# New places for all stages in the engines' orders of a two-layer kernel

## The reference, cut to what matters

```python
xn = layernorm(x)
x = x + cosformer(xn) + ffn0(xn)    # 16 heads of 8; linear attention
                                    # ffn0: 2 shared experts of width 64, 16 routed ones, top 4, gelu
xn = layernorm(x)
x = x + attention(xn) + ffn1(xn)    # causal softmax attention, 16 heads of 8, rotary places
                                    # ffn1: 8 experts of width 512, top 1:
# y = (silu(x @ w1[e][:, :512]) * (x @ w1[e][:, 512:])) @ w2[e] * max_prob
```

## Time and profile before

| what | value |
| --- | --- |
| median of the runs shown | 1367.89 us |
| profiled execution: its own time by its span | 1371.5 us |
| TensorE busy | 1209.3 us, 88% |
| VectorE busy | 991.5 us, 72% |
| ScalarE busy | 912.8 us, 67% |
| GpSimd busy | 692.6 us, 50% |

### The profile page before, as it was taken

How to read it: one execution, slowest core, us unless ns; L and a number is a source line. 1 busy time by engine, 2 the same in 40 slices (tenths; PEclk the granted TensorE clock), 3 DMA queues, 4 the chain that set the end, 5 groups by cost and what they waited for, 6 DMA issues and landing times.

```text
span 1371.5 us, 28942 instructions
## 1 busy us (share of the span) xinstructions
PE 1209.3 (88%) x10216; PEld 700.1 (51%) x10216; DVE 991.5 (72%) x2378; ACT 912.8 (67%) x1233; POOL 692.6 (50%) x1093
## 2 busy tenths in 40 slices
PE   2675999999999999999999999999986999899990
PEld 1342445445454545454454545454432476799990
DVE  2163888888888988888888989888868462344545
ACT  1141777778687868777786877787773667577760
POOL 6324455554536464554545464655543345466760
PEclk9898999999999999999999999999996799999995
DMA  7323505050524416060515335060615210111118
GB/s 224 63 57 64 111 19 115 20 103 27 96 53 71 91 32 120 11 115 20 103 34 88 72 52 105 19 120 14 111 37 171 74 29 25 31 48 50 50 48 250
DMA packets 80300, 100.90 MB, mean 74 GB/s; under 512 B 8800, under 2 KB 56672, under 8 KB 79776
## 3 DMA queue, kind: packets, MB, share of 16 engines
q1 hardware_dynamic: 75680, 89.85, 29.9%
q0 software_dynamic: 4480, 9.22, 2.3%
HBM read 73.50 MB, written 25.01 MB: 72 GB/s over the span
## 4 chain that ended last, share of the span: by engine, by line
PE 63%; DVE 20%; issue 5%; ACT 4%; POOL 4%; DMA 3%; ACTq 0%; SPq 0%; DVEq 0%; POOLq 0%
PE PS L628 9%; PE PS L595 8%; PE PS L440 7%; PE PS L484 7%; PE PS L561 5%; PE PS L639 4%; PE PS L580 4%; PE PS L423 4%; DVE xn L824 3%; PE PS L434 2%; DVE nm L985 2%; DMA early<-gate_rows 2%; PE PS L462 2%; PE PS L570 2%; DVE ra L933 1%
## 5 line engine op out<-in xcount | busy, mean ns | idle before, releaser
L735 ACT ACTIVATE flow<-PS 128x1024 f32<-128x1024 f32 x320 | 321.2, 1028 | 129.4 <-PE PS L580 112.1
L1146 POOL TENSOR_SCALAR_AFFINE_SELECT flow<-flow 128x256 f32<-128x256 f32 (+1 forms) x448 | 191.0, 444 | 374.3 <-ACT flow L735 371.7
L595 PE MATMUL PS<-flow 128*32 128x512 f32 (+3 forms) x2048 | 181.2, 455 | 6.2 <-POOL flow L1146 6.2
L985 DVE TENSOR_REDUCE nm<-PS 128x2 f32<-128x1024 f32 x128 | 154.6, 1220 | 42.3 <-PE PS L549 38.9
L1133 POOL TENSOR_TENSOR early<-early 128x512 f32<-128x512 f32 x128 | 160.7, 1270 | 20.9 <-DMA early<-gate_rows 20.0
L484 PE MATMUL PS<-early,down 128*128 128x512 f32 x288 | 151.8, 637 | 18.4 <-POOL early L1133 17.9
L726 ACT COPY qp<-PS 2x1024 f16<-2x1024 f16 x128 | 128.5, 1004 | 51.0 <-PE PS L570 49.8
L440 PE MATMUL PS<-xnT,up 128*128 128x512 f32 x288 | 152.6, 625 | 3.7 <-DVE at L908 3.4
L987 DVE TENSOR_REDUCE nm<-PS 128x2 f32<-128x768 f32 x128 | 121.6, 950 | 32.4 <-PE PS L549 32.3
L628 PE MATMUL PS<-xsT,w1s 128*128 128x128 f32 x1152 | 141.5, 276 | 3.0 <-DVE act L1079 2.9
L1076 DVE SCALAR_TENSOR_TENSOR tanh<-tanh,PS 128x512 f32<-128x512 f32 x72 | 49.5, 687 | 130.0 <-ACT tanh L769 130.0
(11 more groups left out here) (178 smaller groups left out, 2263.3 us busy)
## 6 DMA issues: line engine op xcount, KB each, us to landing
early<-gate_rows SPq DMA_DIRECT2D x32, 1024.0 KB, 10.8
qp<-relay_q SPq DMA_DIRECT2D x64, 128.0 KB
kp<-relay_k SPq DMA_DIRECT2D x64, 128.0 KB
xsb<-xs SPq DMA_DIRECT2D x76, 64.5 KB, 1.8
relay_k<-qkh SPq DMA_DIRECT2D x32, 128.0 KB, 2.3
early<-in_w SPq DMA_DIRECT2D x1, 4096.0 KB, 14.8
out_y<-X SPq DMA_DIRECT2D x4, 1024.0 KB, 7.9
relay_q<-qkh SPq DMA_DIRECT2D x16, 128.0 KB, 2.3
```

The lines of the kernel that those rows point to most:

```text
L595: ins = pe.matmul(m.PS[32 * j:32 * j + 32, m.PV, kt * P:], m.vst[b % 2][:, kt, 4 * g + j, :], m.pt[:, r, k * L + o:k * L + o + L - kt * P] ...
L735: act.activation(m.pt[:, n % RING, :], m.PS[:, i:i + 2, :].rearrange("p k c -> p (k c)"), ACT.Exp, scale=1.0 / SCALE).then_inc(s["exp"], 1)
L985: dve.tensor_reduce(nm[:, 3, 2 * n:2 * n + 2], ps, AX_X, ALU.max, negate=True).then_inc(s["max"], 1)
L1146: ins = pool.affine_select(part, part, [[0, part.shape[1]], [1, P]], ALU.is_ge, nothing, base=0, channel_multiplier=-1)
```

## The change

Only numbers change. Every place in FIRST, SECOND, ATTENTION and LAST is new. In LAST the formula `tile(n)` is gone: each stage of each of the 72 tiles has a place of its own, and `NBETWEEN` is written as 21, which is what the formula gave. No instruction is added or removed in the stages' functions; the order in which an engine comes to them is another. Table loads on ScalarE are put in by the compiler where gelu follows exp or the other way round, so their number follows from the order.

```diff
 FIRST = placed(
-    xnT0=[-47.65],
-    kvr=[-46, -45.65, -45.5, -44.4],
-    q=[-41.75],
-    kv=[-41.6],
-    route0=[-43.7],
-    gate=[-41.3],
-    attn0=[-40.4],
-    gT=[-40.05],
-    at0T=[-39.05])
+    xnT0=[-51.8],
+    kvr=[-50.2, -46.13, -45, -43.45],
+    q=[-43.68],
+    kv=[-42.11],
+    route0=[-43.17],
+    gate=[-42.42],
+    attn0=[-41.31],
+    gT=[-41.28],
+    at0T=[-35.6])
 SECOND = placed(
-    rope=[-24.3, -23.3],
-    relay=[-20],
-    logits=[-23.65],
-    route1=[-20.45],
-    sort=[-18.25, -17.5, -14.95, -13.45])
+    rope=[-24, -22.99],
+    relay=[-18.34],
+    logits=[-21.9],
+    route1=[-21.61],
+    sort=[-20.26, -18.9, -18.78, -18])
 ATTENTION = placed(
-    mparts=[-2.85, 3.3, 8.15, 10.35],
-    mrows=[-0.85, 5.2, 10.4, 12.1],
+    mparts=[-2.44, 3.7, 7.79, 10.27],
+    mrows=[-1.75, 4.84, 9.09, 11.23],
...
-LAST = [(-19.5, "w1", 0), (-4.5, "w2", 0), (-13, "spares", 0)] + [(-12.4 + 1.2 * k, "tables", k) for k in range(6)]
-LAST += [(-11, "pads", 0)] + [(-5, "load", n) for n in range(U)]
-TILE0, STEP = 0, 1.3
-LAST += [(tile(n) + 0.05, "load", n + U) for n in range(NTILE)]
-LAST += [(tile(n - 1) - 0.5, "staged", n) for n in range(NTILE)] + [(tile(n - 1) + 0.3, "rows", n) for n in range(NTILE)]
-LAST += [(tile(n - 1) - 0.15, "turned", n) for n in range(NTILE)] + [(tile(n), "hidden", n) for n in range(NTILE)]
-LAST += [(tile(n + 1) + 0.15, "outputs", n) for n in range(NTILE)]
+LAST = placed(
+    w1=[-36.12],
+    w2=[-18.1],
+    spares=[-10.55],
+    tables=[-13.25, -11.18, -10.55, -8.9, -7.92, -6.83],
+    pads=[-18.1],
+    load=[-16.83, -16.3, -14.92, -10.94, -9.21, ...
+    hidden=[-1.79, -0.6, 1.63, 4.29, 5.01, 6.3, ...
+    outputs=[0.1, 1.63, 4.41, 5.66, 6.34, 7.83, ...
```

More of the change, by code:

```diff
@@ L117 @@
 FIRST = placed(
-    stats0=[-57.35],
-    norm0=[-49.85],
-    xnT0=[-47.65],
-    kvr=[-46, -45.65, -45.5, -44.4],
-    up=[-43, -40.85, -39.8, -38.8, -38.75, -36.4, -36.15, -35.2, -35],
-    q=[-41.75],
-    kv=[-41.6],
-    route0=[-43.7],
-    gate=[-41.3],
-    attn0=[-40.4],
-    gT=[-40.05],
-    at0T=[-39.05])
-SECOND = placed(
[L131 to L136, removed]
-    rope=[-24.3, -23.3],
-    parts=[-23.55, -22.35],
-    relay=[-20],
-    v=[-19.2],
-    logits=[-23.65],
-    route1=[-20.45],
-    expert=[-19.65],
-    ranks=[-17.05],
-    sort=[-18.25, -17.5, -14.95, -13.45])
@@ L146 @@
-ATTENTION = placed(
[L147 to L150, removed]
-    mparts=[-2.85, 3.3, 8.15, 10.35],
-    mrows=[-0.85, 5.2, 10.4, 12.1],
[L153 to L157, removed]
@@ L161 @@
-LAST = [(-19.5, "w1", 0), (-4.5, "w2", 0), (-13, "spares", 0)] + [(-12.4 + 1.2 * k, "tables", k) for k in range(6)]
-LAST += [(-11, "pads", 0)] + [(-5, "load", n) for n in range(U)]
-TILE0, STEP = 0, 1.3
-def tile(n):
-    return TILE0 + STEP * n
-LAST += [(tile(n) + 0.05, "load", n + U) for n in range(NTILE)]
-LAST += [(tile(n - 1) - 0.5, "staged", n) for n in range(NTILE)] + [(tile(n - 1) + 0.3, "rows", n) for n in range(NTILE)]
-LAST += [(tile(n - 1) - 0.15, "turned", n) for n in range(NTILE)] + [(tile(n), "hidden", n) for n in range(NTILE)]
@@ L173 @@
-LAST += [(tile(n + 1) + 0.15, "outputs", n) for n in range(NTILE)]
-NBETWEEN = sum(tile(n) < max(at for at, *_ in ATTENTION) + 2 * STEP for n in range(NTILE))
+    stats0=[-57.94],
+    norm0=[-52.55],
+    xnT0=[-51.8],
+    kvr=[-50.2, -46.13, -45, -43.45],
+    up=[-43.29, -42.41, -40.15, -38.87, -38.37, -36.06, -35.68, -35.11, -34.61],
+    q=[-43.68],
[5 more added lines that the diff above has]
+    at0T=[-35.6])
+SECOND = placed(
+    down=[-34.96, -33.64, -32.87, -32.2, -31.59, -29.85, -29.73, -28.74, -28.67],
+    gated=[-37.65, -35.56, -35.36, -34.6, -34.45, -34.21, -32.58, -31.95],
+    x1=[-28.23],
+    stats1=[-27.57],
+    norm1=[-26.3],
+    xnT1=[-25.05],
+    rope=[-24, -22.99],
+    parts=[-23.31, -21.8],
+    relay=[-18.34],
+    v=[-16.2],
+    logits=[-21.9],
+    route1=[-21.61],
+    expert=[-20.88],
+    ranks=[-17.82],
+    sort=[-20.26, -18.9, -18.78, -18])
@@ new lines @@
+ATTENTION = placed(
+    score=[-0.43, -0.39, 1.8, 3.41, 6.65, 7.79, 8.64, 9.73, 11.6, 11.63, 12.33, 12.67, 13.98, 14.18, 14.71, 15.24,
+           15.28, 16.29, 17.45, 18.67],
+    max=[-9.15, -8.98, -7.2, -3.75, -2.67, -1.58, 0.83, 0.98, 1.69, 3.44, 3.96, 4.2, 4.52, 4.54, 5.16, 5.34, 6.39,
+         7.62, 9.01, 9.44],
+    mparts=[-2.44, 3.7, 7.79, 10.27],
+    mrows=[-1.75, 4.84, 9.09, 11.23],
+    value=[2.84, 7.31, 9.24, 11.69, 12.35, 13.45, 14.56, 15.46, 17.21, 17.25, 18.77, 19.91],
+    sums=[13.47, 20.12],
+    heads=[14.87, 21.92],
+    mT=[23.92],
+    out=[24.26])
@@ new lines @@
+LAST = placed(
[4 more added lines that the diff above has]
+    pads=[-18.1],
+    load=[-16.83, -16.3, -14.92, -10.94, -9.21, -8.83, -6.73, -6.41, -6.28, -4.77, -4.76, -1.09, -0.52, -0.27, 1.03,
[4 rows of a table added]
+    staged=[-3.94, -3.43, -1.17, 0.17, 2.93, 4.48, 5.22, 6.21, 7.03, 9.22, 9.68, 10.69, 11.68, 14.61, 14.65, 15.08,
[4 rows of a table added]
+    rows=[-4.59, -4.27, -1.28, 0.85, 3.36, 4.48, 5.51, 8.1, 10.41, 11.86, 12.32, 13.47, 14.02, 14.23, 17.05, 17.63,
[4 rows of a table added]
+    turned=[-3.94, -2.04, -0.59, 1.46, 4.01, 5.07, 6.64, 6.93, 7.14, 8.4, 10.04, 12.56, 13.46, 13.76, 15.47, 18.12,
[4 rows of a table added]
+    hidden=[-1.79, -0.6, 1.63, 4.29, 5.01, 6.3, 7.08, 8.08, 9.29, 10.71, 11.71, 13.61, 14.91, 15.89, 18.12, 18.91,
[4 rows of a table added]
+    outputs=[0.1, 1.63, 4.41, 5.66, 6.34, 7.83, 9.37, 9.69, 12.23, 14.19, 14.95, 16.12, 18.21, 19.23, 20.2, 21.81,
[4 rows of a table added]
@@ L178, in stages @@
+NBETWEEN = 21
 def stages():
```

## The result

The changed kernel takes 1401.78 us (median of 4 runs, 1395.39 to 1407.77) against 1368.39 us (1367.87 to 1370.34) for the kernel before: 1.0236 times as long, 95% interval 1.0200 to 1.0272. The forecast was 1359 us with a range of its own from 1349 to 1365, and the range over all rivals went from 1339 to 1377 us, so the result lies beyond every value that was named. The profiled execution took 1399.01 us; the rows are from it. First the page's head: the span, the engines' busy time, and the TensorE clock in 40 slices.

The account below looks back on a forecast made before the run. TensorE was taken to bound the equal periods, with VectorE close behind and pacing the tables' stretch. Terms of -1 (periods), -3 (start), -3.5 (tables) and -1.5 (tiles) summed to -9 us: 1359 us, range 1349 to 1365.

Parts of the forecast that it names:

- The equal periods: Repeating periods from 161 to 1001 us: net 0.0 to -0.1 us per period, -1 us over 13.5.
- The 1.44 us to be won: Per period, TensorE's waits at mrows3 (1.06 us) and value4 (0.38 us) both go.
- The new waits: Per period, the denser order adds waits at attn0 (0.5), max9 (0.6) and norm0 (0.3 us), 1.4 us in all.
- the bracket: VectorE's stretch from rope0 to kv: 12.1 us if kv gets 1.0 us back, 13.1 us if not.
- The slower rival: VectorE's rope0-to-kv stretch runs longer beside GpSimd's q; attn0 waits 1.8 us, +1.25 us per period, 1377 us; chance 0.18.
- Table loads: ScalarE, per period: six loads become eight, 2.6 us more, hidden as a sum but showing at max9 as 0.6 us.
- The tiles: Woven and lone tiles: -1.5 us, from one 1.22 us wait at H20 or its successor and 0.8 us filled at O71.
- a ragged tile costs nothing while this holds: Tiles: uneven order is free if H has its product and staged weights, and O comes 2.0 us or more after H.
- The rival of ragged tiles: Tiles: if one in four waits 1.2 us, as H20 does, 51 tiles give 15 us: 1375 us; chance 0.08.
- The start: Batch 1: sorts before gated1 and work between downs shorten waits such as down5's 1.35 us: -3 us, ends 0 and -5.
- The tables' stretch: Where tables are made: VectorE's waits for route1's exp (2.12 us) and the last sort's transfer (2.50 us) shrink: -3.5 us.
- the woven tiles: Tiles woven into the last attention, 1085 to 1190 us: gains and losses of under 1 us.

Follow-up runs that it names:

- loads6: Changed kernel with up0 of the next batch but two moved next to up1, for six table loads per period instead of eight: 1393.63 us (1.0185).
- both_thin: Changed kernel with GpSimd's products with the gates, and q's two multiplications from batch 1 on, cut to one column: 1327.12 us (0.9692).
- fix_max: Kernel before with max0 and max1 of the next batch placed ahead of mrows3: 1357.13 us (0.9914).
- fix_both: Kernel before with max0 and max1 ahead of mrows3 and value4 behind down5: 1395.59 us (1.0180).
- gate_first: Kernel before with only the gate moved ahead of kv on VectorE: 1410.44 us (1.0280).
- fix_both_norm: Kernel before with max0 and max1 ahead of mrows3, value4 behind down5 and norm0 moved behind max1: 1356.72 us (0.9904).

## Why the prediction was wrong

The reading of what bounds the kernel held: the change mainly opened and closed gaps of TensorE. The errors are in the terms.

**The equal periods: -1 us forecast, +28.8 measured.** This is the step that failed. The 1.44 us to be won came as put. The new waits were put at 0.5 (attn0), 0.6 (max9) and 0.3 us (norm0), 1.4 in all. They came to 1.09, 0.38 and 1.16, with kv0's 0.81 and mrows2's 0.54 that no step named and about 0.2 us each at value11 and two downs. The working used each of VectorE's durations as the trace of before had it, apart from one: I took 1.0 us off kv because it would leave GpSimd's q behind. That was right (kv fell from 1.77 to 0.77 us). Another 1.05 us came back at route0 (1.52 to 0.47), which the sum did not have: its subtraction had run beside a third kind of multiplication, the rotation's, which the working never looked at:

```profile
576.17 1.27 POOL L1151 TENSOR_TENSOR ra<-ra,rb 128x512 f32<-128x512 f32 x1 [1.23 <-DVE rb L935]
```

So 2.1 us were won. But q's multiplications had only moved: they now fall on kvr3 (1.26 to 2.20 us) and on the parts of rope0 (0.67 to 1.78), which costs 2.1 us and delays rope1's eviction, hence kv0's wait. The stretch from rope0 to kv took 12.83 us, between the 12.1 and 13.1 of the working: the bracket held by luck, since 1.05 us that it did not have were won at route0 and 2.1 us that it did not have were lost. For norm0 the row with its 3.1 us was not read at all; a place among five products made it 4.21, and mparts2 behind it went from 1.27 to 1.59. The forecast saw the toll in the earlier trace rows and treated it as a property of one instruction, where it belongs to a moment.

**The slower rival** named kvr3 beside q's multiplications, which came true, but priced only attn0, at 1.8 us, with a net of 1.25 us per period. Attn0 waited 1.09, kv got its 1.0 us back, and moving the gate back behind kv gave 0.1 us per period, so the gate's place alone did not decide.

**Table loads.** Two more per period, as forecast. Max9's wait of 0.38 us was put at 0.6. It did not go when the loads did (loads6: 0.40), so the loads are not shown to be its cause. The Trainium skill's 2.66 us per switch ("ScalarE: Activation LUTs", What ACT_TABLE_LOAD costs) is made of 1283 ns for the load and a drain of some 1380 ns. The traces have the 1283 ns and not the drain: from the end of the activation before a load to the start of the one behind it pass 1.31 us (median of 118 in the changed kernel).

**The tiles: "a ragged tile costs nothing while this holds" failed**, +14.4 us from H22 to H70 (3.09 us per tile; the sign set for it was 2.80). The rival of ragged tiles had 15 us and a chance of 0.08, for a reason, a tile in four waiting for the act, that is not what happens. From 1230 to 1362 us TensorE's waits are:

```profile
PE PS L643 <- DMA xsb<-xs: 3.6, 4, 1.2
PE PS L662 <- issue: 2.5, 5, 0.6
PE PS L662 <- DVE act L1102: 0.5, 1, 0.5
```

The count of buffers that the step rested on left out the gathers (`load`): a load placed late makes T wait for its DMA, up to 1.2 us. It also took stages' lengths from the even order. In a ragged order O follows T or another O directly, and in five such places it starts 0.2 to 0.6 us late without a releaser that the profile shows (`issue`). Gaps sum to 8.0 us, and 6.4 us more are slower advance without a gap, such as 0.95 us from O to the H behind it, where O to the T behind it is 0.89 in the even order. Why these are slower stays open. Even steps gave back 12.6 us. The two small gains that this term held came as put: -1.6 us up to H22 and -1.1 us at the end, against -1.5 in all.

**The start: -3 forecast, -0.2 measured**, within its ends of 0 and -5. Down5's wait of 1.35 us went as forecast, but the products with the gates of batch 1 begin 1.5 us later than before (110.78 against 109.30 us), as their gates land later, and end 1.1 us earlier (120.61 against 121.70) instead of 2.2; kv0 of that stretch has a new wait of 2.0 us.

**The tables' stretch and the woven tiles** together gained 14.1 us where -3.5 and under 1 us were put. The windows over the three periods with the tables in them, by the marks of the table above (before, then after), show nearly the same busy time and shorter gaps, 21.0 instead of 25.3 us of them:

```profile
901.27:1084.43 183.16, 157.87 (x1411) 72.74 (x1410) 142.80 (x319) 121.71 (x147) 84.85 (x133) 0.88 0.40 95
```

```profile
929.96:1108.36 178.40, 157.39 (x1449) 75.95 (x1445) 140.28 (x320) 126.69 (x151) 85.81 (x137) 0.90 0.40 98
```

Two hidden stages more are done in it. Both waits of VectorE went as the step said, the 2.12 us for route1's exp to 0.65 and the 2.50 us for the sort's transfer to nothing. In the last attention the gaps fell from 9.5 to 5.8 us; why was not tried. The last attention's gain needs the batch's table and the tiles' table together: with either of before it takes 112.1 or 118.4 us.

What stays open: the share of GpSimd's own queue in both_thin's gain, what the same cut gives in the kernel before, what set the last attention's gaps, the slower advance in ragged tiles, and a version of the changed kernel that keeps its 16 us of gains with periods of 61.5 us, which was not tried.

## What to carry to other kernels

Before costing a reorder, list the operations whose duration in the trace is several times that of a twin of the same shape, and find what runs beside them on the neighbour engine. Here their excess was a toll on a moment: in the new order give it to whatever small operation stands there, and ask who waits for that one. A wait that vanishes is worth its time only if the engine behind it has become earlier, and one change of place that closes a known gap (fix_max, -12 us) can be worth more than a whole new table.

## What the runs showed of the hardware

- Where one of VectorE's TENSOR_SCALAR or TENSOR_TENSOR operations from SBUF to SBUF starts beside a GpSimd multiplication of 1.23 to 1.28 us, it ends behind the end of one, the small ones of 0.2 to 0.3 us by less than 0.1 us: norm0's four instructions in the changed kernel end at 562.99, 564.23, 565.46 and 566.68 us, the products at 562.91, 564.15, 565.37 and 566.59 (in quiet the four take 1.10 us); the larger qkl (0.67 us in quiet) ends 0.5 us behind. It need not be the first product: one instruction lasted over masks, a product, masks and another product, 3.96 us, in fix_both. Reductions from PSUM do not stretch (1211 to 1227 ns, all 128 in the kernel before), a RECIPROCAL in SBUF took 0.18 us beside a product in gate_first (412.25 us) as it does in quiet, and norm1, in part beside GpSimd's masks, took 1.20 us in fix_max. That VectorE and GpSimd share their SBUF access is in the Trainium skill ("GPSIMD Engine Reference", Specifications), which names contention for instructions with two SBUF inputs or in a 2-port mode; the size is from the rows here. The trace agrees for an instruction with two SBUF inputs (px in gate_first, 0.22 to 1.02 us); norm0 and kv's long operation have one tensor input there, and no row shows their mode.
- A wait of TensorE of about 2 us can be followed at once by a record of 3.4 us at the 1.2 GHz level: twelve of them in fix_both. It need not be: in gate_first attn0 waits 2.3 us in each of 12 periods, and there are five records. The changed kernel has more idle time per period, in smaller pieces, and three such records (at 212, 407 and 861 us); the kernel before, loads6, both_thin and fix_both_norm have none in their periods. In fix_both each costs about 12 x 1.50 / 11 = 1.6 us on top of the wait.
- The changed kernel's four runs spread over 12.4 us, and their mean granted clock differs: 0.959 and 0.955 in the runs of 1399.01 and 1395.39 us, 0.946 and 0.944 in those of 1404.56 and 1407.77. So the two slower runs spent more time at the 1.2 GHz level; where in the program is on record for the profiled run alone. The kernel before keeps 0.956 to 0.961 in the 40 runs beside the experiments, which spread over 9.4 us.
